# Attention outputs stored by feature with their softmax sums apart, and a regrouped cross-attention prologue, in a two-layer transformer kernel

## The reference

```python
def _attn(x, ctx, wq, wk, wv, wo, bo, heads):
    ...
    sim = jnp.einsum('bhid,bhjd->bhij', q, k) * scale
    a = jax.nn.softmax(sim, axis=-1)
    out = jnp.einsum('bhij,bhjd->bhid', a, v)
    out = out.transpose(0, 2, 1, 3).reshape(b, n, heads * dh)
    return out @ wo + bo
h1 = _ln(x, n1_g, n1_b)
x = _attn(h1, h1, q1, k1, v1, o1_w, o1_b, heads) + x
h2 = _ln(x, n2_g, n2_b)
x = _attn(h2, context, q2, k2, v2, o2_w, o2_b, heads) + x
h3 = _ln(x, n3_g, n3_b)
...
ff = a * jax.nn.gelu(g, approximate=False) @ ff_w2 + ff_b2
return ff + x
```

## Time and profile before

| what | value |
|---|---|
| median of 3 runs | 3340.49 us (3337.49 to 3342.36) |
| the profiled execution, its own time | 3342.7 us |
| its span, first to last instruction | 3341.0 us |
| mean granted clock of TensorE | 0.841 |
| busy share of PE, DVE, ACT, POOL | 88%, 65%, 57%, 24% |

### The profile page before, as it was taken

The page is one execution under the profiler, slowest core; times in us unless marked ns, Lnnn a source line. Parts: engine busy times, 40 slices in busy tenths (PEclk is TensorE's granted clock), DMA queues, the critical chain, the costliest instruction groups (busy, mean ns, idle before and its releaser), DMA issues. The chain is left out here.

```text
span 3341.0 us, 47964 instructions
## 1 busy us (share of the span) xinstructions
PE 2936.9 (88%) x15594; PEld 1775.7 (53%) x15594; DVE 2157.7 (65%) x3834; ACT 1892.4 (57%) x3214; POOL 805.5 (24%) x1149
## 2 busy tenths in 40 slices
PE   6989999978696999998959999879978577899999
PEld 5754444457455888886731111111126342788888
DVE  5668888837453444444649999968868685444443
ACT  4328888844353232233549999989975355333322
POOL 2021221114640000000027888200003471200000
PEclk9969999989798999998975555555559898899999
DMA  8663333336762000001567557266723213010000
GB/s 228 211 166 101 106 107 103 90 80 158 165 176 46 10 10 19 9 0 38 152 173 163 128 137 164 32 90 83 97 56 96 79 45 92 26 36 18 25 17 16
DMA packets 358243, 296.57 MB, mean 89 GB/s; under 512 B 175602, under 2 KB 281914, under 8 KB 358058
## 3 DMA queue, kind: packets, MB, share of 16 engines
q1 hardware_dynamic: 347994, 273.93, 34.0%
q0 software_dynamic: 7280, 18.07, 2.1%
q10 hardware_dynamic: 2784, 2.29, 0.4%
HBM read 177.53 MB, written 114.52 MB: 87 GB/s over the span
## 5 line engine op out<-in xcount | busy, mean ns | idle before, releaser
L1591 PE MATMUL nat<-k_stack,q_stack 48*128 48x512 bf16 x640 | 381.0, 605 | 71.5 <-DMA k_stack<-k1w 31.1
L1391 DVE TENSOR_REDUCE neg_max<-nat 128x1 f32<-128x512 f32 x640 | 400.7, 682 | 61.3 <-PE nat L1250 61.2
L1625 DVE TENSOR_REDUCE m_all<-nat 128x1 f32<-128x512 f32 x640 | 423.3, 691 | 18.1 <-PE nat L1591 17.8
L804 POOL TENSOR_TENSOR rstd<-var_eps,neghalf 128x4 f32<-128x4 f32 x48 | 51.9, 1081 | 1588.0 <-DVE var_eps L1028 1588.0
L1645 ACT ACTIVATE nat<-nat,m_all 128x512 f32<-128x512 f32 x640 | 427.7, 2130 | 3.0 <-DVE m_all L1625 2.9
L1645 ACT ACTIVATION_READ_ACCUMULATOR nat<-nat,m_all 128x1 f32 x640 | 403.6, 1674 | 0.0
L1054 DVE SCALAR_TENSOR_TENSOR ff<-outp,bias,gel 128x512 f32<-128x512 f32 x160 | 120.1, 751 | 417.6 <-PE outp L326 417.6
L1325 ACT ACTIVATE probs<-sT 128x1024 f32<-128x1024 f32 x320 | 328.0, 1027 | 93.1 <-PE sT L1259 85.5
L968 ACT ACTIVATE gel<-outp,bias 128x512 f32<-128x512 f32 x160 | 110.0, 688 | 351.6 <-PE outp L326 351.6
L1839 ACT ACTIVATE exps<-sT 128x1024 f32<-128x1024 f32 x320 | 293.4, 1573 | 10.5 <-PE sT L1788 10.5
L972 ACT CAST ff_hi<-ff 128x512 fp32r<-128x512 f32 x160 | 99.2, 620 | 312.3 <-DVE ff L1054 312.3
(11 more groups left out here) (561 smaller groups left out, 7163.3 us busy)
## 6 DMA issues: line engine op xcount, KB each, us to landing
v<-vpad SPq DMA_DIRECT2D x64, 320.0 KB, 2.8
q_stack<-q_part SPq DMA_DIRECT2D x90, 160.0 KB, 5.8
k_stack<-k1w SPq DMA_DIRECT2D x90, 160.0 KB, 10.5
q_stack<-q_hi SPq DMA_DIRECT2D x160, 64.0 KB, 2.5
v_stack<-v SPq DMA_DIRECT2D x40, 256.0 KB, 3.2
q_stack<-q_hi SPq DMA_DIRECT2D x80, 128.0 KB, 2.8
raw<-v SPq DMA_DIRECT2D x16, 640.0 KB, 14.9
k_stack<-k_hi SPq DMA_DIRECT2D x158, 64.0 KB, 2.2
```

What stands on the lines that cost most here:

```text
L1391: dve.tensor_reduce(neg_max[:, n % 2, qt, 2 * pr + ab:2 * pr + ab + 1], nat[(16 * (n + 2) + t) % 3][:, :], AX.X, ALU.max, negate=True).the ...
L1591: pe.matmul(bank[i % NAT][:, :], q_stack[half, slot, g, pr, qt * P:(qt + 1) * P], k_stack[half, slot, g, pr, :], start=True, stop=True).th ...
L1625: dve.tensor_reduce(k.m_all[:, column(i // TILES, i % TILES)], bank[i % NAT][:, :], AX.X, ALU.max, negate=True).then_inc(s["e_max_ready"], 1)
```

## The change

Four things change, all in the first layer.

1. `self_attention`: `turn_output`, its copy, its reciprocal and `norm` go. `o_sb` has two slots; ACT copies `o_ps` of group n-2 into slot n % 2; POOL stores it from there with five DMAs, the four rows of sums to `self_sums` and four times 16 rows to `self_out`, which now lies by feature. When a sample's five groups are stored, SP loads its sums back as 80 rows of 128 (`load_sums`), DVE takes the reciprocal (`invert`), POOL splits it into a high and a low part, and SP stores these to `self_shares`. The block no longer waits for its stores at its end.
2. `dense_phase` with `main="q"` reads by feature. Three new steps `scale` per sample: PE multiplies the 40 rows of shares (20 high, 20 low) by a constant pattern `spread`, which gives each of 128 features its head's share, and DVE multiplies the loaded outputs by it in place.
3. `cross_attention`: queries are loaded for two groups at once (pairs), the columns of the parts are ordered so that one DMA writes the shift rows, POOL's loader has 4 jobs with a turn in every fourth group, and the early bias is added in the last 32 groups instead of the first.
4. The other 6 weight jobs go to the start of the feed-forward stage, on POOL.

The diff, cut to its core (unchanged context and renamed counts left out):

```diff
-def self_attention(nc, s, k, q, kk, v, out, next_weights, bias):
+def self_attention(nc, s, k, q, kk, v, out, sums_dram, recips, next_weights, bias):
...
+        o_sb = sb("o_sb", [P, 2, TOK])
+        sums, shares = (k.m_all[0:TT * HEADS, P * i:P * i + P] for i in range(2))
+        share_hi, share_lo = (k.s_all[0:TT * HEADS, P * i:P * i + P].bitcast(F32R) for i in range(2))
...
+                def load_sums(b):
+                    for r in range(2):
+                        wait(sp, f"b_o_stored{r}", 80 * ((QUADS * (b + 1) - r + 1) // 2))
+                    sp.dma_start(sums, rows(sums_dram, b * HEADS, HEADS).rearrange("h (x t) -> h x t", t=P)
+                                 ).then_inc(s["a_sums_loaded"], 16)
+
+                def store_shares(b):
+                    wait(sp, "a_share_split", 2 * b + 2)
+                    for i, half in enumerate((share_hi, share_lo)):
+                        sp.dma_start(rows(recips, (2 * b + i) * HEADS, HEADS).rearrange("h (x t) -> h x t", t=P),
+                                     words(half)).then_inc(s["a_recip_stored"], 16)
...
-                for n in range(-2, NQ + 3):
+                for n in range(-2, NQ + 7):
...
-                    if exists(n - 3):
-                        wait(sp, "a_o_normed", n - 2)
-                        sp.dma_start(rows(out, (n - 3) * TOK, TOK).rearrange("(t p) c -> p t c", p=P),
...
+                    if exists(n - 4) and (n - 4) % QUADS == QUADS - 1:
+                        load_sums((n - 4) // QUADS)
+                    if exists(n - 7) and (n - 7) % QUADS == QUADS - 1:
+                        store_shares((n - 7) // QUADS)
...
-                for r in range(2):
-                    wait(sp, f"a_o_stored{r}", 16 * (NQ // 2))
...
-                        if exists(n - 2) and j == 2:
-                            turn_output(n - 2)
...
                     if exists(n - 2):
                         wait(act, "a_pv_done", n - 1)
-                        wait(act, "a_turn_full", output_use(n - 3) + 1 if n > 2 else 0)
-                        act.copy(o_sb[:, :], o_ps[:, :]).then_inc(s["a_o_copied"], 1)
+                        wait(act, f"b_o_stored{n % 2}", 80 * (n // 2 - 1))
+                        act.copy(o_sb[:, n % 2, :], o_ps[:, :]).then_inc(s["a_o_copied"], 1)
...
-                        if exists(n - 2) and j == 2:
-                            wait(act, "a_turn_full", output_use(n - 2) + 1)
-                            wait(act, "a_o_normed", n - 3)
-                            act.copy(o_turned[:, n % 2, :], output_bank(n - 2)).then_inc(s["a_turn_free"], 1)
...
+                def store(n):
+                    wait(pool, "a_o_copied", n + 1)
+                    done = s[f"b_o_stored{n % 2}"]
+                    pool.dma_start(rows(sums_dram, n * 4, 4), o_sb[DH:P:VCOL, n % 2, :]).then_inc(done, 16)
+                    for h in range(4):
+                        pool.dma_start(rows(out, (4 * n + h) * DH, DH), o_sb[VCOL * h:VCOL * h + DH, n % 2, :]
+                                       ).then_inc(done, 16)
+
+                def split_shares(b):
+                    wait(pool, "a_recip", b + 1)
+                    wait(pool, "a_recip_stored", 32 * b)
+                    pool.tensor_copy(share_hi, shares).then_inc(s["a_share_split"], 1)
+                    wait(pool, "a_share_split", 2 * b + 1)
+                    pool.tensor_tensor(share_lo, shares, share_hi.bitcast(F32), ALU.subtract
+                                       ).then_inc(s["a_share_split"], 1)
...
                     wait(pool, "a_parts_ready", n + 1)
-                    if n >= 4:
-                        norm(n - 4)
+                    if n >= 5:
+                        store(n - 5)
+                    if n > 2 * QUADS and n % QUADS == 2:
+                        split_shares(n // QUADS - 2)
                     loader.turn(pool, n)
                     if n < BATCH * TT:
                         early.add(pool, n)
-                for n in range(NQ - 4, NQ):
-                    norm(n)
+                for n in range(NQ - 5, NQ):
+                    store(n)
+                for b in (BATCH - 2, BATCH - 1):
+                    split_shares(b)
...
+                def invert(b):
+                    wait(dve, "a_sums_loaded", 16 * (b + 1))
+                    wait(dve, "a_share_split", 2 * b)
+                    dve.reciprocal(shares, sums).then_inc(s["a_recip"], 1)
...
+                        if t == 8 and exists(n - 5) and (n - 5) % QUADS == QUADS - 1:
+                            invert((n - 5) // QUADS)
```

In `dense_phase`:

```diff
-            body = [("stats", 0), *oT[0:2], items[0], oT[2], ("norm", 0), items[1], items[2], oproj[0], ("double", 0),
+            if scale:
+                ahead["scale"] = 2
+            body = [("stats", 0), *scale, *oT[0:2], items[0], oT[2], ("norm", 0), items[1], items[2], oproj[0], ("double", 0),
...
+                        pe.matmul(bank_of(st, r)[:, :], spread[:, m * P:(m + 1) * P], shares[:, :], start=True, stop=True
+                                  ).then_inc(s[turned[st][0] + "_full"], 1)
...
+                        dve.tensor_tensor(attn[:, m, :], attn[:, m, :], bank_of(st, r)[:, :], ALU.mult
+                                          ).then_inc(s[turned[st][0] + "_drained"], 1)
```

In `cross_attention` and where the stages are called:

```diff
-                        sp.dma_start(words(q_stack[32 * quadrant:32 * quadrant + 32, n % RING]),
-                                     rows(q[part], n * 64, 64).rearrange("(x r) t -> r x t", r=32)
-                                     ).then_inc(s[f"x_q_loaded{n % RING}"], 16)
+                        sp.dma_start(words(q_stack[32 * quadrant:32 * quadrant + 32, 2 * r:2 * r + 2]
+                                           ).rearrange("r u x t -> r (u x) t"),
+                                     rows(q[part], pair * 128, 128).rearrange("(y r) t -> r y t", r=32)
+                                     ).then_inc(s[f"x_q_loaded{r}"], 16)
...
-                        for pr in range(2):
-                            act.dma_start(words(q_stack[QROWS:ROWS, (n + 2) % RING, pr, :]),
-                                          words(shift_sb[6 * pr:6 * pr + 6, n % 2, :])
-                                          ).then_inc(s[f"x_shift_loaded{n % 2}"], 16)
+                        act.dma_start(words(q_stack[QROWS:ROWS, (n + 2) % RING, :, :]), words(shift_sb[0:12, n % 2, :])
+                                      ).then_inc(s[f"x_shift_loaded{n % 2}"], 16)
...
-                    loader.turn(pool, n)
-                    if n < BATCH * TT:
-                        early.add(pool, n)
+                    if n % 4 == 3 and n // 4 <= len(loader.jobs):
+                        loader.turn(pool, n // 4)
+                    if n >= NQ - BATCH * TT:
+                        early.add(pool, n - (NQ - BATCH * TT))
...
             dense_phase(nc, s, k, 0, "q", w["n2_g"], w["n2_b"], [wq], wo, self_out, stores={"q": q20},
-                        next_weights=[w1])
+                        next_weights=[w1], by_feature=True, recips=self_shares,
+                        recips_stored="a_recip_stored")
...
             dense_phase(nc, s, k, 0, "ff", w["n3_g"], w["n3_b"], [w1, *w2], wo2, cross_out,
-                        ff_bias=(w["ff_b1"], w["ff_b2"]))
+                        ff_bias=(w["ff_b1"], w["ff_b2"]), next_weights=w2[1:])
```

144 lines of the change are left out of this document (79 added, 65 removed).

## The result

The changed kernel takes **3675.07 us** (median of 4 runs, 3671.57 to 3676.86); the kernel before, run beside it, 3341.43 (3337.49 to 3347.41). The ratio is **1.0994**, 95% interval 1.0979 to 1.101: slower by 334 us, where the forecast said 255 more. The profiled execution took 3675.4 us, its span is 3673.7 us, 332.7 us more than before.

A forecast was written before the change was run, and what follows sets the result against it. It took PE, ACT and DVE to hold one another in a ring with little slack. Terms +180 + 82 - 4 + 4 - 2 - 5 = +255 us gave 3597.7, as a median 3596 us; range 3500 to 3690, forecast 3530 to 3700.

The forecast's parts named there:

- The mechanism: Self-attention: ACT's copy into `o_sb` waits for a store landing; loops of 16.69 us, 5.13 more than 11.56.
- The term of +180: Self-attention, store behind the copy: 35 loops (4 to 38) at 5.13 us more each, 180 us; ends 162 and 201.
- the loops without a stall: Self-attention loops 0 to 3 and 39: each saves 0.77 us of PE, 4 us less in all.
- S: Start of L1362 in a self-attention loop, where POOL begins its parts; the forecast's delay is counted from it.
- The clock: Self-attention: PE's stall drops the clock; 5.5 low us of work cost 2.35 us a loop, 82 us in all.
- turn to S: Self-attention: step from PE's turn of shifts to the next S, 10.10 less 0.77, so 9.33 us.
- never back: Rival: self-attention clock never returns to full rate, 242 us instead of 82, total 3756; chance 0.08.
- no loss: Rival: self-attention stalls but PE keeps 2.4 GHz, sum without 82, total 3514; chance 0.17.
- The dense stage: Three products replace twelve transposes, DVE gains 2.25 us per sample: 2 us less, -13 to +6; wrong if moved over 15.
- The border: Last self-attention copy to SP's first dense load: 9.3 us instead of 5.4, 4 us more; 2 to 7.
- Cross-attention: First eight group intervals take 41.0 us where 27.6 would do; 5 us less taken, -9 to +2.
- Copies 18 to 20 us apart: Sign of being right: spacing of ACT's copies into `o_sb`, with a self-attention stage of some 750 us instead of 502.

The follow-up runs named there:

- experiment 1: Changed kernel with POOL storing group m-4 in iteration m instead of m-5, the stores one group earlier; 3349.6 us, ratio 1.0019.
- experiment 7: Changed kernel with POOL's store of group n - 5 ahead of the parts of the shifts instead of behind them; 3631.94 us, ratio 1.0867.
- experiment 6: Changed kernel with 6 unused 128-row products on PE in each stalled self-attention loop, ahead of the turn of the shifts; 3549.29 us, ratio 1.063.
- experiment 3: Kernel before with only the change's cross-attention part and its moved feed-forward weight jobs; 3335.03 us, ratio 0.9978.
- experiment 8: Changed kernel with stores one group earlier and a sample's first two dense scale products moved to the end of the round before; 3336.76 us, ratio 0.9982.
- experiment 9: Changed kernel with stores one group earlier and no scaling in the dense stage, so outputs go undivided into the projection; 3315.82 us, ratio 0.9918.
- 10: Changed kernel with early stores, two scale products a round forward, and the cross-attention's first two groups' queries loaded one by one; 3335.42 us, ratio 0.9984.
- 11: Kernel before with the change's cross-attention part, but the first two groups' queries loaded singly; 3335.19 us, ratio 0.9983.
- experiment 4: Changed kernel with 22 unused 48-row products on PE in each stalled self-attention loop, ahead of the turn of the shifts; 3706.47 us, ratio 1.108.
- experiment 2: Changed kernel with the third scale product of a dense round moved behind the first query product; 3671.43 us, ratio 1.0966.

## Why the prediction was right, and where it was short

**The mechanism was the one named:** ACT's wait for `self_out` in 35 loops and none in experiment 1; path steps of 5.30 and 1.66 us for 5.71 and 1.65; a shorter loop when the parts leave the path (experiment 7, though only 0.7 us of it on the path itself); and a mean loop of 16.7 us at a clock of 0.98 for 16.69 (experiment 6). The term of +180 with -4 for the loops without a stall measured +177. In the loop shown, from S to the last issue it was 3.4 us (1.40 to the first DMA, 0.60 for it, three times 0.48) for 3.31; from that issue to the copy 1.9 for 2.4. The rule of the Trainium skill, "DMA: Bandwidth & Descriptors", section "Anatomy of one DMA — SWDGE (gpsimd) path", by which this landing was an estimated 2.1 us, was nearer than the 2.4 taken from the earlier trace rows; over the 116 such DMAs between 300 and 900 us the median is 2.2.

**The clock was mis-sized: +82 forecast, +124 measured.** The step that fell short is "I take 5.5 low us of work per loop". It was 9.5 in the loop shown (window 678.80 to 692.50) and 8.8 on the mean of the 35, near the upper end of 10.1 that one restart in the earlier trace rows had shown; I had taken a value between that and a 3.4 us stretch that held no stall. At 0.43 lost of each, 9.5 gives 4.1 us, and turn to S is indeed 4.1 us longer than 9.33 in that loop. By the mean it is 3.8 us a loop, 132 in all; experiment 6, which keeps the clock up in 34 of the loops, gives back 124. In seven loops the work at half rate was 3.3 to 5.7 us, and these are the short ones. The rival "never back" (242) and the rival "no loss" (0) are both out. What the prediction quoted from the Trainium skill, "TensorE: Matmul & The Clock Gate", section "HAM oscillation — how this bites in real kernels", that each piece of work between such waits starts cold, is what the trace shows: behind each of the 35 stalls PE starts at 0.50, the granted clock of the stage is 0.69, and it is 0.98 once the stall is filled.

**The dense stage was wrong in sign: -2 forecast, +30 measured** between its rounds (the 4 us behind the last round go with the start of the cross-attention, where experiment 3 finds them too). That is twice the 15 us from which on, by the prediction's own words, it would be wrong. It added up DVE's work (2.25 us of multiplications, 3 x 0.69 = 2.1 measured) against PE's transposes and asked for no order. What the order does: of the 4.3 us by which a round grew on the mean, some 2 are the multiplications, which stay in experiment 8 and go in experiment 9, and 2.2 are PE's wait for the bank and the clock behind it, which go in experiment 8. The credit for the transposes, read from another layer's 13.8 us, hardly exists (experiment 9).

**The border** took 9.6 us more instead of 4. Of the chain from the last copy to SP's first load (996.2 to 1011.5, 15.2 us; 5.4 in the earlier trace rows) all but the end was in the sum:

```profile
1003.21 0.95 DVE L1425 RECIPROCAL m_all<-m_all 80x128 f32<-80x128 f32 x1 [26.98 <-DMA m_all<-self_sums]
...
1005.06 0.80 SPq L1260 DMA_DIRECT2D self_shares<-s_all  x2
...
1011.49 0.30 SPq L688 DMA_DIRECT2D shares<-self_shares  x1
```

Up to the end of SP's stores at 1005.9 it is 9.6 us, with 9.3 forecast; the 5.6 us from there to the first load were not counted. They are the end of the block, for which all engines wait, and POOL comes last: its drain takes 6.70 us (1004.5 to 1011.2) where it took 0.63 before. No run shows why it is so long; it is the same 6.70 us in experiments 1 and 9.

```profile
L1235 POOLq DRAIN  x1: 6697/6697/6697, 1004.5 to 1004.5; - x1
```

Before:

```profile
L1199 POOLq DRAIN  x1: 631/631/631, 699.6 to 699.6; - x1
```

**Cross-attention** gained 12 us between its exponentials for 5 forecast, and lost 4 ahead of them; alone it is worth 7 (experiment 3).

**How far it was luck.** Of the 78 us by which the change cost more than forecast, 43 are the self-attention, nearly all of it the clock, 32 the dense rounds, 6 the border, and 3 were gained at the cross-attention. The range up to 3700 had been drawn for a slow landing and a long stretch of low clock. That 3675 lies within it although the dense stage was far outside its own bounds of -13 to +6 is owed to the width of the range, not to the sum. Copies 18 to 20 us apart and a stage of some 750 us had been named as well; they were 20.1 on the mean and 802.

What now stands against what: the self-attention by feature with early stores gains 27 us, the dense rounds give back 30 and the border 9, and the cross-attention's part gains 7. The best time found with the scaling in place is 0.998 of the kernel before, in four versions (experiments 3, 8, 10 and 11) that the measurement can't tell apart. Two of them, 3 and 11, are the kernel before with the cross-attention's part alone.

## What to carry to other kernels

A ring of two buffers whose store hangs on the consumer's own previous step makes a closed path; count its steps from the issue of the last store, not from its size. When a store or load is issued from an in-order engine, ask in which iteration it stands and what must have happened before that iteration begins: one iteration earlier was worth 325 us here, with no other edit. And when two steps share a ring of banks with an engine that has other work first, place the steps by when that engine comes round, since both the wait and the clock behind it are paid.

## What the runs showed that was not expected

- With 22 products of 48 rows added, PE was busy for 14.68 of 14.70 us and the clock was 0.67 (experiment 4); with six products of 128 rows in the same place the clock was 0.98 over the stage, with PE busy for 500 of 540 us (experiment 6). So here it did not suffice that PE had an instruction at all times. The two kinds of product differ in rows and in type, and which of the two mattered was not separated.
- A 512-column product of 128 rows of plain 32-bit floats came as two instructions of 0.43 us each (12 instructions for six products, 5.42 us together), against some 0.23 us from one to the next for the projection's products of the rounded type (1115.85 to 1116.08 in the changed kernel).
- Adding work that nobody uses made the changed kernel 126 us faster (experiment 6).
- DVE's four normalisations took 3.17 us beside one POOL subtraction, and 1.50 without it (experiment 2). In the kernel before they took 2.66 (at 755.65).
- The drain of POOL at the end of the self-attention took 6.70 us, 0.63 before the change.
